# Gate and up scaled in place in PSUM, another order of the down product, layer norms in the block loop

## The reference

```python
x = x + 0.5 * ffn(layernorm(x))      # x: 2 x 1024 x 512, float32
x = x + s4(layernorm(x))             # a causal convolution over the 512 columns, plus D*x
x = x + 0.5 * ffn(layernorm(x))      # the same weights again

def qlinear(x, q, scale, A, Bm):     # q: integers 0..15
    w = (q - 7.5) * (scale * 0.005)[:, None]
    return x @ w.T + 0.02 * (x @ A @ Bm)          # A, Bm: rank 32
def ffn(x):                          # H = 512, I = 1376
    h = silu(qlinear(x, gate...)) * qlinear(x, up...)
    return qlinear(h, down...)
```

## Time and profile before

| | us |
|---|---|
| median of 3 runs | 646.56 (645.61 to 646.78) |
| the profiled execution | 643.84, its span 642.1 |
| PE busy | 591.5 |
| DVE busy | 455.2 |
| ACT busy | 284.7 |
| POOL busy | 72.1 |

### The profile page before, as it was taken

The page is one execution under the profiler, slowest core; times in us unless marked ns, Lnnn a source line. Parts: engine busy times, 40 slices in busy tenths (PEclk is TensorE's granted clock), DMA queues, the critical chain, the costliest instruction groups (busy, mean ns, idle before and its releaser), DMA issues.

```text
span 642.1 us, 10660 instructions
## 1 busy us (share of the span) xinstructions
PE 591.5 (92%) x3630; PEld 340.7 (53%) x3630; DVE 455.2 (71%) x873; ACT 284.7 (44%) x625; POOL 72.1 (11%) x89
## 2 busy tenths in 40 slices
PE   3898889999999999999886999999999999999997
PEld 2443564446644574455654544664457445754465
DVE  6699876896588758892769589537883688546643
ACT  3774314661266314661383366216641466126630
POOL 4246600000000001000064000000000000000000
PEclk9999899999999999999999999999999999999999
DMA  8982210004000210000078200300021000223001
GB/s 306 395 284 104 50 30 5 1 2 75 8 0 0 53 25 6 2 0 2 18 131 163 36 1 0 72 13 1 0 51 30 4 0 16 58 90 115 1 18 50
DMA packets 67624, 35.52 MB, mean 55 GB/s; under 512 B 56160, under 2 KB 60448, under 8 KB 67584
## 3 DMA queue, kind: packets, MB, share of 16 engines
q1 hardware_dynamic: 66768, 34.87, 20.8%
q10 hardware_dynamic: 816, 0.14, 0.1%
HBM read 17.43 MB, written 4.19 MB: 34 GB/s over the span
## 4 chain that ended last, share of the span: by engine, by line
PE 65%; DVE 13%; ACT 4%; issue 4%; DMA 3%; SPq 1%; POOL 1%; DVEq 0%; ACTq 0%; POOLq 0%
PE bank L1072 36%; PE down_acc L1034 19%; PE bank L1089 5%; DMA PT<-p_stack 2%; DVE work L732 2%; DVE zs L642 1%; DVE work L727 1%; DVE z L649 1%; PE bank L1003 1%; PE bank L1051 1%; PE bank L1145 1%; ACT work L529 1%; ACT hT L534 1%; ACT work L552 1%; DMA xT<-z 1%
## 5 line engine op out<-in xcount | busy, mean ns | idle before, releaser
L1034 PE MATMUL down_acc<-dw,hT 128*128 128x320 f16 (+3 forms) x1408 | 187.8, 288 | 6.6 <-DVE hT L671 6.6
L529 ACT ACTIVATE work<-bank,scales 128x512 f32<-128x512 f32 (+1 forms) x176 | 120.4, 685 | 128.0 <-PE bank L1072 127.6
L1072 PE MATMUL bank<-xT,gw 128*128 128x512 f16 (+1 forms) x696 | 164.4, 379 | 1.2 <-ACT work L529 0.8
L1072 PE MATMUL bank<-xT,uw 128*128 128x512 f16 (+1 forms) x696 | 164.4, 379 | 0.0
L1034 PEld LDWEIGHTS down_acc<-dw,hT 128*128 128x128 f16 (+1 forms) x1408 | 135.7, 99 | 45.9 <-DVE hT L671 9.2
L1072 PEld LDWEIGHTS bank<-xT,gw 128*128 128x128 f16 (+1 forms) x696 | 68.9, 100 | 81.7 <-ACT work L529 1.8
L1072 PEld LDWEIGHTS bank<-xT,uw 128*128 128x128 f16 (+1 forms) x696 | 69.6, 100 | 78.9
L714 DVE SCALAR_TENSOR_TENSOR work<-bank,work 128x512 f32<-128x512 f32 (+1 forms) x88 | 60.6, 688 | 29.6 <-ACT work L529 20.8
L727 DVE SCALAR_TENSOR_TENSOR work<-bank,work 128x512 f32<-128x512 f32 (+1 forms) x88 | 60.5, 687 | 26.1 <-ACT work L529 25.8
L732 DVE TENSOR_TENSOR work<-work 128x512 f32<-128x512 f32 (+1 forms) x88 | 63.6, 723 | 4.6 <-ACT work L552 1.3
L671 DVE SCALAR_TENSOR_TENSOR hT<-work,hT 128x512 f16<-128x512 f32 (+1 forms) x88 | 60.7, 690 | 6.1 <-ACT hT L534 5.6
(11 more groups left out here) (150 smaller groups left out, 429.1 us busy)
## 6 DMA issues: line engine op xcount, KB each, us to landing
out_x<-X SPq DMA_DIRECT2D x16, 256.0 KB, 2.1
X<-in_x SPq DMA_DIRECT2D x1, 2048.0 KB, 14.6
gq_raw<-in_tables SPq DMA_DIRECT2D x1, 2048.0 KB, 11.4
gq_raw<-in_gate_q_t SPq DMA_DIRECT2D x2, 768.0 KB, 11.3
uq_raw<-in_up_q_t SPq DMA_DIRECT2D x2, 768.0 KB, 11.4
dq_raw<-in_down_q_t SPq DMA_DIRECT2D x1, 1536.0 KB, 14.3
work<-in_b SPq DMA_DIRECT2D x2, 688.0 KB, 8.5
X<-in_x SPq DMA_DIRECT2D x4, 256.0 KB, 5.1
```

The costliest lines, as they stand in the source:

```text
L529: return nc.scalar.activation(out, in_, ACT.Copy, scale=scales[0:rows[m], g, m:m + 1])
L1034: last = mm(down_acc[b][:, c, 0:width], hT[0:rows[m], m, a, j * P:(j + 1) * P], dw[0:rows[m], m, c, 0:width], start=(m == 0 and a == 0), s ...
L1072: last = mm(dst[0:r, :], w[:, c, cols], xT[:, a, c, :], start=(c == 0 and a == 0), stop=(c == KH - 1 and a == 1))
```

## The change

`scaled` writes the product back into its own PSUM bank; the low-rank matmul then adds onto it there (`start=False`). The gate uses banks 0 and 2 in turn, up banks 1 and 3. silu and h read PSUM directly, with the scale of the sum in silu and in the split of h; tg, tu, g32 and u32 are gone. PE issues the low-rank matmuls of a block behind the products of the next, those of the last block inside the down product. The down product takes groups 0 and 1 together: both halves over blocks 0 to 8, then the last two blocks. The next pass's statistics are at m = 1 to 4 and all four applications at m = 5 to 8. The transfers of z wait for the last up product, those of p also for the last low-rank matmul, and all z transfers go before all of p. `down_pass`, `h_ready` and POOL's code are as before.

```diff
@@ -320,15 +324,17 @@
             .then_inc(f.xT[j], 16)
     else:
         sp.wait_ge(f.p_stack, n * TS + j + 1)
+        sp.wait_ge(f.ul_mm, n * M)
         sp.sem_inc(s_released, 1)
         sp.dma_start(PT[:, :, cols], p_stack[:, j % 2, :, :, :].rearrange("p g a r -> p (g a r)"),
                      transpose=True).then_inc(f.PT[j % 2], 16)
 def transposes(n):
-    sp.wait_ge(f.ul_mm, n * M)
-    for what, j in ("x", 0), ("x", 1), ("x", 2), ("p", 0), ("x", 3), ("p", 1), ("p", 2), ("p", 3):
-        transpose(n, what, j)
+    sp.wait_ge(f.u_mm, n * M)
+    for what in "xp":
+        for j in range(TS):
+            transpose(n, what, j)
 def conv_transpose(i):
...
@@ -525,45 +531,60 @@
                          bank[bank_t][:, :].bitcast(F16).rearrange("p (a k t) -> p a k t", a=2, k=KH),
                          ACT.Copy).then_inc(f.xT0, 1)
-def scaled(out, in_, g, m):
-    return nc.scalar.activation(out, in_, ACT.Copy, scale=scales[0:rows[m], g, m:m + 1])
+def scaled(acc, g, m):
+    return nc.scalar.activation(acc, acc, ACT.Copy, scale=scales[0:rows[m], g, m:m + 1])
 def h_high(n, m):
     b, r = m % 2, rows[m]
     act.wait_ge(f.h[b], uses(n, m) + 1)
-    nc.scalar.activation(hT[0:r, m, 0, :], h32[0:r, b, :], ACT.Copy, scale=H_SCALE)\
+    nc.scalar.activation(hT[0:r, m, 0, :], h32[0:r, b, :], ACT.Copy, scale=H_SCALE * LR_OUT)\
         .then_inc(f.hhi[b], 1)
+def gate_silu(n, m):
+    b, r = m % 2, rows[m]
+    act.wait_ge(f.gl_mm, n * M + m + 1)
+    after(act, f.h[b], uses(n, m))
+    nc.scalar.activation(silu[0:r, b, :], gate_bank[b][0:r, :], ACT.Silu, scale=LR_OUT)\
+        .then_inc(f.silu[b], 1)
 def tile(n, more, s4=False):
     for m in range(M):
-        b, r, k = m % 2, rows[m], uses(n, m)
+        b, r = m % 2, rows[m]
         act.wait_ge(f.g_mm, n * M + m + 1)
-        after(act, f.g[b], k)
-        scaled(tg[0:r, b, :], bank[0][0:r, :], 0, m).then_inc(f.tg[b], 1)
+        scaled(gate_bank[b][0:r, :], 0, m).then_inc(f.tg[b], 1)
+        if m:
+            gate_silu(n, m - 1)
+        act.wait_ge(f.u_mm, n * M + m + 1)
+        scaled(up_bank[b][0:r, :], 1, m).then_inc(f.tu[b], 1)
         if m:
             h_high(n, m - 1)
-        act.wait_ge(f.u_mm, n * M + m + 1)
-        after(act, f.u[b], k)
-        scaled(tu[0:r, b, :], bank[1][0:r, :], 1, m).then_inc(f.tu[b], 1)
-        act.wait_ge(f.g[b], k + 1)
-        after(act, f.h[b], k)
-        nc.scalar.activation(silu[0:r, b, :], g32[0:r, b, :], ACT.Silu).then_inc(f.silu[b], 1)
         if isinstance(n, int) and n == 0 and m in (0, 2, 4):
             cast_up(1 + m // 2)
+    gate_silu(n, M - 1)
     h_high(n, M - 1)
-    for j in range(TS):
-        pd_high(n, j)
-        pd_copy(n, j)
+    pd_high(n, 0)
+    pd_high(n, 1)
+    pd_copy(n, 0)
+    if s4:
+        act.wait_ge(s_toep, 1)
+        nc.scalar.activation(toep[:, :], bank[0][:, :], ACT.Copy).then_inc(s_tcopy, 1)
+    for j in range(2):
         if more:
             p_high(n + 1, j)
-        if s4 and j == 1:
-            act.wait_ge(s_toep, 1)
-            nc.scalar.activation(toep[:, :], bank[0][:, :], ACT.Copy).then_inc(s_tcopy, 1)
-        if s4 and j == 2:
-            for i in range(2):
-                conv_norm(i)
+    pd_copy(n, 1)
+    pd_high(n, 2)
+    if more:
+        p_high(n + 1, 2)
+    pd_copy(n, 2)
+    if s4:
+        for i in range(2):
+            conv_norm(i)
+    pd_high(n, 3)
+    if more:
+        p_high(n + 1, 3)
+    pd_copy(n, 3)
     if s4:
         for i in range(2, AHEAD):
             conv_norm(i)
...
@@ -668,7 +689,7 @@
 def h_low(n, m):
     b, r = m % 2, rows[m]
     dve.wait_ge(f.hhi[b], uses(n, m) + 1)
-    V.scalar_tensor_tensor(hT[0:r, m, 1, :], h32[0:r, b, :], H_SCALE, hT[0:r, m, 0, :],
+    V.scalar_tensor_tensor(hT[0:r, m, 1, :], h32[0:r, b, :], H_SCALE * LR_OUT, hT[0:r, m, 0, :],
                            ALU.mult, ALU.subtract).then_inc(f.hlo[b], 1)
 def down_read(n, j):
...
@@ -703,16 +724,15 @@
                         ALU.add, ALU.mult).then_inc(c_var, 1)
 def tile(n, base, more, s4=False):
-    c = LR_SCALE / (P_SCALE * B_SCALE)
     k0 = (n + 1) * TS
     x0 = k0 - base * TS
     for m in range(M):
         b, r, k = m % 2, rows[m], uses(n, m)
-        dve.wait_ge(f.tg[b], k + 1)
-        dve.wait_ge(f.gl_mm, n * M + m + 1)
-        after(dve, f.silu[b], k)
-        V.scalar_tensor_tensor(g32[0:r, b, :], bank[2][0:r, :], c, tg[0:r, b, :],
-                               ALU.mult, ALU.add).then_inc(f.g[b], 1)
+        dve.wait_ge(f.ul_mm, n * M + m + 1)
+        dve.wait_ge(f.silu[b], k + 1)
+        after(dve, f.hlo[b], k)
+        V.tensor_tensor(h32[0:r, b, :], silu[0:r, b, :], up_bank[b][0:r, :], ALU.mult)\
+            .then_inc(f.h[b], 1)
         if m:
             h_low(n, m - 1)
         if isinstance(n, int) and n == 0 and m == 1:
...
@@ -721,22 +741,11 @@
             down_b()
         if isinstance(n, int) and n == 0 and m == 4:
             down_a()
-        dve.wait_ge(f.tu[b], k + 1)
-        dve.wait_ge(f.ul_mm, n * M + m + 1)
-        after(dve, f.h[b], k)
-        V.scalar_tensor_tensor(u32[0:r, b, :], bank[3][0:r, :], c, tu[0:r, b, :],
-                               ALU.mult, ALU.add).then_inc(f.u[b], 1)
-        dve.wait_ge(f.u[b], k + 1)
-        dve.wait_ge(f.silu[b], k + 1)
-        after(dve, f.hlo[b], k)
-        V.tensor_tensor(h32[0:r, b, :], silu[0:r, b, :], u32[0:r, b, :], ALU.mult)\
-            .then_inc(f.h[b], 1)
-        if more and m in (1, 3, 6, 8):
-            j = (1, 3, 6, 8).index(m)
-            ln_stats(k0 + j, j, x0 + j)
-        if more and m in (5, 7):
-            j = (5, 7).index(m)
+        if more and m in range(1, 1 + TS):
+            ln_stats(k0 + m - 1, m - 1, x0 + m - 1)
+        if more and m in range(1 + TS, 1 + 2 * TS):
+            j = m - 1 - TS
             ln_apply(n + 1, j, x0 + j)
         if s4:
...
@@ -751,31 +760,36 @@
             if m in (6, 8):
                 s4_phase(m - 6, m - 4)
     h_low(n, M - 1)
+    pd_split(n, 0)
+    down_read(n, 0)
+    pd_split(n, 1)
     if more:
-        for j in (2, 3):
-            ln_apply(n + 1, j, x0 + j)
-    for j in (0, 1):
-        pd_split(n, j)
-        if more:
-            p_split(n + 1, j)
-        down_read(n, j)
-        down_add(n, j, base)
+        p_split(n + 1, 0)
+    down_read(n, 1)
+    down_add(n, 0, base)
     if s4:
         s4_diagonal()
         s4_maximum()
+    if more:
+        p_split(n + 1, 1)
+    down_add(n, 1, base)
     if isinstance(n, int) and n == 0:
         s4_vectors()
         s4_inverse(0)
-    for j in (2, 3):
-        pd_split(n, j)
-        if more:
-            p_split(n + 1, j)
-        down_read(n, j)
-        down_add(n, j, base)
-        if s4 and j == 2:
-            s4_split()
-            conv_low(0)
-            conv_low(1)
+    pd_split(n, 2)
+    if more:
+        p_split(n + 1, 2)
+    down_read(n, 2)
+    down_add(n, 2, base)
+    if s4:
+        s4_split()
+        conv_low(0)
+        conv_low(1)
+    pd_split(n, 3)
+    if more:
+        p_split(n + 1, 3)
+    down_read(n, 3)
+    down_add(n, 3, base)
     if s4:
         conv_low(2)
         conv_low(3)
...
@@ -1054,51 +1068,46 @@
...
+    def product(g, m):
+        b, r, cols = m % 2, rows[m], slice(m * P, m * P + rows[m])
+        w, dst, done = ((gw, gate_bank[b], f.g_mm), (uw, up_bank[b], f.u_mm))[g]
+        after(pe, (f.silu, f.h)[g][b], uses(n, m))
+        if m == 0 and g == 1:
+            pe.wait_ge(f.p_stack, n * TS + TS)
+        if m == 0 and g == 0 and not (isinstance(n, int) and n == 0):
+            pe.wait_ge(s_bread, 1)
+        if m == 1 and g == 0:
+            after(pe, f.dsum, n * TS)
+        if isinstance(n, int) and n == 0:
+            pe.wait_ge((s_gcast, s_ucast)[g], 1 + sum(m >= m1 for _, m1 in CHUNKS))
+        for c in range(KH):
+            for a in range(2):
+                last = mm(dst[0:r, :], w[:, c, cols], xT[:, a, c, :],
+                          start=(c == 0 and a == 0), stop=(c == KH - 1 and a == 1))
+        last.then_inc(done, 1)
+
+    def low_rank(g, m):
+        b, r, cols = m % 2, rows[m], slice(m * P, m * P + rows[m])
+        w, dst, done = ((gb_w, gate_bank[b], f.gl_mm), (ub_w, up_bank[b], f.ul_mm))[g]
+        pe.wait_ge((f.tg, f.tu)[g][b], uses(n, m) + 1)
+        if m == 0 and g == 0:
+            if isinstance(n, int) and n == 0:
+                pe.wait_ge(f.PT0, TS)
+            else:
+                for b_pt in range(2):
+                    pe.wait_ge(f.PT[b_pt], n * 32)
+        if isinstance(n, int) and n == 0 and m == 0:
+            pe.wait_ge(s_bw, g + 1)
+        mm(dst[0:r, :], w[:, cols], PT[:, g, :], start=False, stop=True,
+           skip_group_check=True).then_inc(done, 1)
+
+    started = first and n == 0
+        for g in range(2):
+            if not (started and m == 0):
+                product(g, m)
+            if m:
+                low_rank(g, m - 1)
...
@@ -1108,24 +1117,49 @@
             pe.wait_ge(out_read, SUBS // TS)
```

(115 more changed lines are left out.)

## The result

The changed kernel takes 653.1 us (median of 4 runs, 650.8 to 653.8), the kernel before 646.1 beside it: ratio 1.0103, interval 1.0074 to 1.0133. It is slower by 7.0 us; 652.5 was forecast. The profiled execution took 653.83 us with a span of 652.1, the longest of its four, so the traces differ by 10.0 us where the medians differ by 7.0. Run again among the experiments the kernel took 653.3 us against 645.1 (1.0127, 1.0102 to 1.0153).

A forecast was written before the change was run, and what follows sets the result against it. PE, busy 92% of the span, was taken as the bound, so only its gaps counted: gaps closed minus gaps opened summed over the passes to +6.0 us, added to the median 646.56 for 652.5 us, range 644.5 to 656.5.

The forecast's parts named there:

- The block-8 wait: Start of each down product: PE waits 1.54 us for the low half of block 8, eight times, 12.3 us.
- What closes: PE gaps expected to go: PT 6.1 us, low halves of h 6.6 us, first pd_stack waits 2.7 us; VectorE work freed.
- the first pd_stack wait: Before the pd_stack transpose, passes 1 to 6: VectorE free of the layer norm; 7 waits lose 2.7 us.
- pd_stack of group 2: PE waits for its split behind VectorE's additions: about 1.1 us in passes 1 and 2, 4.2 in pass 0.
- PdT: ScalarE's p copies run ahead of pd_copy: PE waits 0.16 us for group 1, 0.28 for group 2 without a transpose wait.
- The Cauchy wait: Pass 3: Cauchy matmuls wait for s4_resolvents behind h(1) and h_low(0) on VectorE; 2.7 us of new wait, once.
- silu(0): Pass 0 start: holds the gate bank for block 2 behind the cast and 1.28 us table load; PE waits 2.1 us.
- Pass 0's first down wait: Down product in pass 0: ln_apply(3) waits for POOL's rstd ahead of h(9) and h_low(8); PE waits near 4 us.
- The clock: PE's half clock in pass 0: one stretch kept from the earlier trace, making matmuls 1.7 us longer.
- That rival: PE's clock falls more often, 1.7 us per further fall; one to four more give 654 to 659 us; chance 0.10.
- The rule weighed there: Skill's rule: throttled is default, recent PE activity releases it; both gaps of about 4 us in pass 0 likely cost clock.
- In place in PSUM: ScalarE's in-place PSUM operation taken as 0.685 us; up to about 1.0 us costs nothing; dearer adds +9 or more.

The follow-up runs named there:

- the late ask: Changed kernel with PE waiting for the low half of block 8 at m = 8 instead of m = 0: 637.2 us, 0.9878 of the kernel before.
- the order back: The late ask kernel with the down product group by group as before the change, block 10's low-rank matmuls in front: 640.6 us against 637.2.
- the moved vectors: Changed kernel with the S4 vectors except the bank read, and half the inverse, behind pass 0's last addition: 646.8 us.

## Why the prediction was right, and where not

**The block-8 wait** was right in place, number of times and cause, and it decides the sign of the result. In order of time, pass 2, PE and VectorE:

```profile
216.83 0.38 PE L1101 MATMUL bank<-PT,ub_w 128*128 128x512 f16 x1
...
217.41 0.69 DVE L734 TENSOR_TENSOR work<-work,bank 128x512 f32<-128x512 f32 x1 [0.95 <-PE bank L1101]
218.01 0.68 DVE L692 SCALAR_TENSOR_TENSOR hT<-work,hT 128x512 f16<-128x512 f32 x1
...
218.84 2.60 PE L1048 MATMUL down_acc<-dw,hT 128*128 128x320 f16 x18 [1.63 <-DVE hT L692]
```

From the low-rank matmul's start to the down product it is 2.01 us, forecast 1.76, mostly because h starts 0.58 us after that start and not 0.42. Less the matmul's own 0.22 this is 1.79 us a pass and not 1.54, and 1.8 us is what the late ask gave back in such a pass. So eight waits cost more than the forecast 12.3 us. The late ask shows the cause by taking it away.

**What closes** was right in what it listed: PT (6.1 us), the last blocks' halves (6.6 us; only block 8's is left), the first pd_stack wait. The cause given for the last, that VectorE is free of the layer norm, is not needed: with the layer norms back behind the loop these waits stay away in passes 1 to 6 as well, and with the order back and the norms moved they stay away too. Each of the two parts is enough. **pd_stack of group 2**: 0.80 us in passes 1 and 2 (forecast 1.14) and 4.0 in pass 0 (4.2); the order of VectorE's queue is the cause, as the moved vectors show. **PdT**: 0.22 to 0.30 us in the second FFN, as forecast. **The Cauchy wait**: 2.58 (2.7). **silu(0)** behind the table: 2.05 (2.1).

**Pass 0's first down wait** was forecast at 4 us and is 2.9, and its cause was a wrong step: "its rstd comes from POOL behind `s4_norms_real`". In the changed kernel:

```profile
64.38 0.90 POOL L383 TENSOR_TENSOR rstd<-veps,minus_half 128x1 f32<-128x1 f32 x1
...
65.37 1.12 DVE L692 SCALAR_TENSOR_TENSOR hT<-work,hT 128x512 f16<-128x512 f32 x1
66.42 0.70 DVE L663 TENSOR_SCALAR zs<-X,meanvar,rstd 128x512 f32<-128x512 f32 x1
```

The rstd was done 1.1 us before VectorE came to `ln_apply(3)`. VectorE was late by itself, through the operations that POOL's work stretched; I had this only as a slower `ln_apply`. That the down product starts at 69.4 us in the trace where the clock held at 30 us, as forecast, is luck; PE was ready for it at 66.4 and not at 65.4, which is why the wait is shorter. The Trainium skill ("VectorE: DVE Perf Modes", "Two Vector instructions with no wait between them") says that the second operand in SBUF, or the input of a two-port mode, is read through an interface shared with GpSimd; the traces agree, with 0.43 us against 0.79 to 1.37 for the cast, 0.69 against up to 1.64 for the subtraction, and h with an operand in PSUM at 0.68.

**The clock** is the term that was mis-sized. I carried one stretch of half clock over from before (1.7 us, in both sums) and gave 0.10 to more of them. The profiled run has six stretches; the further ones cost 3.4 us in pass 0 and 3.2 in pass 3. Of the 10.0 us between the traces this leaves 3.4 for waits and work, where all of the forecast's 6.0 was waits and work: pass 0 was 0.8 us better than forecast without the clock, passes 1 and 2 together 0.7, pass 3 0.8. That rival is what happened, at 653.1 just under its band of 654 to 659, since the rest came out smaller. That forecast and median agree within 0.6 us is luck: against the trace on which the sum was built, the clock came out 6.6 us dearer and waits and work 2.6 us cheaper, and the medians happen to lie 3 us nearer to each other than the two traces.

The rule weighed there, that the clock follows how busy PE has been lately, was the better guide for the large gaps: those of 2.6, 2.9 and 4.0 us were each followed by half clock in both traces of the changed kernel, the 2.1 us one in one of two. Over all 14 traces, in passes 0 to 3 from 24 us on, half clock began within 1.5 us of the end of all 21 gaps of 2.5 us or more, and of 6 of the 17 between 1.8 and 2.3 us. None of the single waits of 1.4 to 1.6 us ahead of a down product was followed by it; three waits of 1.0 to 1.1 us within 4 us were once, in the kernel with the order back.

**In place in PSUM** costs nothing here: the operation is shorter than into SBUF, and the list of the changed kernel has no wait of PE for it. ScalarE's groups, after, against 685 ns in the earlier trace rows:

```profile
L535 ACT ACTIVATE bank<-bank,scales 128x512 f32<-128x512 f32 x160 | 105.8, 662 | 112.7 <-PE bank L1085 112.3 <-DVE ub_w L809 0.4
...
L547 ACT ACTIVATE work<-bank 128x512 f32<-128x512 f32 x80 | 47.1, 589 | 0.0
```

## What to carry to other kernels

When an engine's turn begins with a new wait, everything that stood later in that turn is now behind the wait, also for consumers whose own wait was not edited: look for semaphores that count work of the turn before. Ask for a result where it is read, not at the head of the group that will read it; here one moved wait was worth 16 us and turned a slower kernel into a faster one. Price a gap on TensorE of 2.5 us or more above its own length, one near 2 us at some chance of it (6 of 17 here), and only where TensorE is busy behind it: in the convolution half clock cost next to nothing. Count moves into a stretch where GpSimd is at work at the stretched duration.

## What was not expected of the hardware

Ten superfluous matmuls in a 2.6 us gap made the kernel 3.2 us faster. Half clock lasted 6.8 us in pass 3 though PE was busy for 6.43 of them, and one stretch stayed when the gap was filled; what ends it is open. ScalarE writing PSUM in place took 662 ns, 23 less than into SBUF with the same scales. The Trainium skill ("ScalarE: Activation LUTs", "Step-by-step: what each stage is for") says that ScalarE reaches PSUM faster than SBUF, and the trace agrees. From a low-rank matmul's start VectorE's product started 0.58 us later.
